# Masked attention on one core: q and k staged by token halves, the prologue by token halves, and another handling of the last two sweeps and of the fallback branch

## The reference

```python
def reference(x, adj, Wq, bq, Wk, bk, Wv, bv, Wo, bo):      # x (8, 1024, 512) f32, adj (8, 1024, 1024) int32
    h = maximum(layernorm(x), 0)
    q, k, v = heads(h @ Wq + bq), heads(h @ Wk + bk), heads(h @ Wv + bv)      # 16 heads of 32
    scores = einsum('bhqd,bhkd->bhqk', q, k) / sqrt(32)
    scores = where(adj[:, None] == 0, -inf, scores)
    out = einsum('bhqk,bhkd->bhqd', softmax(scores), v)
    return x + out.transpose(0, 2, 1, 3).reshape(b, s, 512) @ Wo + bo
```

## Time and profile before

| | |
|---|---|
| median of 3 runs | 1936.64 us (1936.35 to 1942.9) |
| the profiled execution, time | 1935.79 us |
| its span | 1933.9 us |
| PE busy | 1854.5 us, 96% |
| DVE, ACT, POOL busy | 79%, 76%, 82% |
| DMA queue of SP | 203.47 MB, 38.1% of 16 engines |

### The profile page before, as it was taken

One profiled execution on the slowest core, in us unless ns is written; L12 is line 12 of the kernel. 1 busy time (PEld: TensorE's weight loads), 2 busy tenths in 40 slices (PEclk: granted clock), 3 DMA queues, 4 the chain that ended last, 5 costly groups with the idle time before them and its releaser, 6 DMA issues.

```text
span 1933.9 us, 35135 instructions
## 1 busy us (share of the span) xinstructions
PE 1854.5 (96%) x13856; PEld 767.9 (40%) x13856; DVE 1534.0 (79%) x1585; ACT 1473.5 (76%) x1772; POOL 1588.5 (82%) x701
## 2 busy tenths in 40 slices
PE   6989999999999999999999999999999999999997
PEld 4334434444344443444433443334344344343432
DVE  6788877887778887788877887778877788777775
ACT  4878886788867988678876788768887688867763
POOL 0988888887987979878889788888889889898873
PEclk9999999999999999999999999999999999999999
DMA  7532363523615335143442335423444224443121
GB/s 236 141 79 75 97 155 88 138 69 98 167 55 142 88 107 156 50 126 93 134 123 75 101 109 133 117 86 88 113 128 131 82 77 120 137 115 97 35 55 45
DMA packets 114136, 206.09 MB, mean 107 GB/s; under 512 B 12848, under 2 KB 16048, under 8 KB 113968
## 3 DMA queue, kind: packets, MB, share of 16 engines
q1 hardware_dynamic: 113104, 203.47, 38.1%
q10 hardware_dynamic: 864, 0.34, 0.1%
HBM read 153.43 MB, written 50.33 MB: 105 GB/s over the span
## 4 chain that ended last, share of the span: by engine, by line
PE 80%; DVE 10%; DMA 4%; ACT 3%; issue 2%; POOL 0%; SPq 0%; DVEq 0%; POOLq 0%; ACTq 0%
PE ps L783 21%; PE ps L770 20%; PE ps L738 14%; PE ps L820 8%; DVE ring L1068 8%; PE ps L752 7%; PE ps L745 7%; DMA k_stack<-k_parts 2%; ACT ring L905 1%; DMA k_parts<-k_part 1%; PE ps L734 1%; PE ps L793 1%; DVE oT_lo L1125 1%; ACT mask L966 1%; DMA ring<-x 0%
## 5 line engine op out<-in xcount | busy, mean ns | idle before, releaser
L1068 DVE TENSOR_TENSOR ring<-ps,mask 128x1024 f32<-128x1024 f32 x1024 | 1217.3, 1217 | 333.2 <-PE ps L770 306.5
L905 ACT ACTIVATE ring<-ring 128x1024 f32<-128x1024 f32 x1024 | 1062.4, 1050 | 236.1 <-DVE ring L1068 225.6
L1285 POOL TENSOR_TENSOR acc<-acc,ring 128x1024 f32<-128x1024 f32 x380 | 902.8, 2403 | 0.4 <-ACT ring L905 0.4
L1285 POOL TENSOR_TENSOR acc<-ring 128x1024 f32<-128x1024 f32 x252 | 608.8, 2427 | 305.0 <-ACT ring L905 300.4
L770 PE MATMUL ps<-q_stack,k_stack 128*128 128x512 f16 x2048 | 608.0, 382 | 49.3 <-DVE ring L1068 38.9
L783 PE MATMUL ps<-ring,v_sb 128*32 128x512 f32 x4096 | 505.9, 600 | 0.0
L770 PEld LDWEIGHTS ps<-q_stack,k_stack 128*128 128x128 f16 x2048 | 157.6, 97 | 415.9 <-DVE ring L1068 232.5
L783 PEld LDWEIGHTS ps<-ring,v_sb 128*32 128x32 f32 x4096 | 107.2, 109 | 263.2 <-issue 232.9
L820 PE MATMUL ps<-acc,ones 128*32 128x512 f32 x1008 | 131.3, 593 | 0.5 <-POOL acc L1285 0.5
L933 ACT ACTIVATE rden<-ps 128x512 f32<-128x512 f32 x64 | 38.3, 598 | 114.1 <-PE ps L820 114.1
L745 PE MATMUL ps<-wv_lo,hT_hi 128*128 128x128 f16 x1024 | 100.3, 219 | 0.0
(11 more groups left out here) (88 smaller groups left out, 1565.4 us busy)
## 6 DMA issues: line engine op xcount, KB each, us to landing
x_in<-x SPq DMA_DIRECT2D x172, 256.0 KB, 2.9
edges<-adjT SPq DMA_DIRECT2D x128, 256.0 KB, 3.8
q_stack<-q_parts SPq DMA_DIRECT2D x124, 256.0 KB, 4.8
k_stack<-k_parts SPq DMA_DIRECT2D x124, 256.0 KB, 4.8
q_parts<-q_part SPq DMA_DIRECT2D x64, 256.0 KB, 2.0
k_parts<-k_part SPq DMA_DIRECT2D x64, 256.0 KB, 2.1
out<-x_in SPq DMA_DIRECT2D x60, 256.0 KB, 2.0
ring<-x SPq DMA_DIRECT2D x4, 512.0 KB, 5.4
```

What stands on the lines that cost most here:

```text
L905: nc.scalar.activation(tile, tile, ACT.Exp, scale=SCALE / UP / UP).then_inc(s["prob_ready"], 1)
L1068: nc.vector.tensor_tensor(ring[:, slot_of(kt, pair), :].rearrange("p (a n) -> p a n", n=HALF), ps_s(j), mask[:, kt:kt + 1, half * HALF:(ha ...
L1285: nc.gpsimd.tensor_tensor(acc[:, group, pair, :], first_of, ring[:, slot_of(kt, pair), :], ALU.add).then_inc(s["sum_done"], 1)
```

## The change

Four parts.

1. **Prologue by token halves.** SP asks for x tiles 0 to 3, Wq, Wk, x tiles 4 to 7, Wv, a mask tile, bo (which leaves ACT's queue), three mask tiles. Statistics, means, rstd, normalising, transposes and projections are done for tokens 0 to 511 and then for 512 to 1023. `early_pair` puts the products with w_lo of q and k behind the other eight groups.
2. **q and k by token halves in every unit.** Each half is stored when its high or low part is there and loaded back by itself: 16 loads of 128 KB and 8 stores of 128 KB in a unit where there were 8 loads and 4 stores of 256 KB. PE waits for the first halves ahead of tile 0, for the second half of k ahead of tile 8, and for the second half of q ahead of tile 16. `PRODUCTS` and the lags of `high` and `low` are as before.
3. **The last two sweeps.** Sweep 62 has POOL's groups A and B again and `BLOCKS` as any other. Sweep 63 has the terms A, 6, 7 and B, where B is kt 4 and 5. Two additions of bo move from tiles (3, 8), (3, 9) to (2, 14), (2, 15). The reduction of `limits` stays ahead of POOL's sums of tile 12.
4. **One block.** The second block is gone: each engine waits for the flag, reads it and branches behind its own work; SP waits for its last stores (`landed`) behind that.

```diff
@@ general_attention
-        block = ctx.enter_context(nc.Block())
-
         def gated(eng, program):
+
+            eng.wait_ge(verdict_taken, 4)
             wanted = eng.value_load(flag, min_val=0, max_val=1)
             with eng.If(wanted > 0):
                 program()
...
             gated(sp, program)
+            landed(sp)
@@ tables
-LAST_BIAS_AT = {(1, 24): 4, (1, 25): 5, (3, 8): 6, (3, 9): 7, (3, 14): 0, (3, 15): 1, (3, 24): 2, (3, 25): 3}
-
-LAST_TERMS = "A4567"
-UNIT_BLOCKS = {6: ("p0", "p1"), 10: ("p2", "p3"), 14: ("p4", "p5", "dA", "d4", "d5"), 18: ("p6", "d6", "p7", "d7")}
-LAST_BLOCKS = {6: ("p0", "p1"), 10: ("p2", "p3"), 14: ("p4", "p5", "dA", "d4", "d5"), 16: ("p6", "d6"), 17: ("p7", "d7")}
+LAST_BIAS_AT = {(1, 24): 4, (1, 25): 5, (2, 14): 6, (2, 15): 7, (3, 14): 0, (3, 15): 1, (3, 24): 2, (3, 25): 3}
+
+LAST_TERMS = "A67B"
+LAST_SUMS_AT = 8
+LAST_BLOCKS = {6: ("p0", "p1"), 10: ("p2", "p3"), 14: ("p4", "p5", "dA"), 16: ("p6", "d6"), 17: ("p7", "d7", "dB")}
...
 def terms_of(V):
-    return LAST_TERMS if V >= LAST_SWEEP - 1 else TERMS
+    return LAST_TERMS if V == LAST_SWEEP else TERMS
...
 def blocks_of(V):
-    return BLOCKS if V < LAST_SWEEP - 1 else UNIT_BLOCKS if V < LAST_SWEEP else LAST_BLOCKS
+    return BLOCKS if V < LAST_SWEEP else LAST_BLOCKS
@@ SP
+            def store_half(kind, hl, half):
+                tokens = slice(half * HALF, (half + 1) * HALF)
+                sp.dma_start(parts[kind][:, hl, tokens], part[kind][:, hl, tokens]).then_inc(s[f"{kind}_{('high', 'low')[hl]}_{half}_stored"], 16)
+
+            def load_half(U, kind, hl, half):
+                tokens = slice(half * HALF, (half + 1) * HALF)
+                sp.wait_ge(s[f"{kind}_{('high', 'low')[hl]}_{half}_stored"], 16 * (U + 1))
                 for quarter, which in enumerate({"q": (0, 1, 0, 1), "k": (0, 0, 1, 1)}[kind]):
                     if which == hl:
+                        sp.dma_start(stack[kind][quarter * DH:(quarter + 1) * DH, U % 2, :, tokens],
+                                     parts[kind][:, hl, tokens].rearrange("(h p) n -> p h n", h=HG))\
+                            .then_inc(s[kind + "_second_half_stacked" if half else "first_half_stacked"], 16)
...
+            load_x_first(0)
+            load_x_first(1)
             load_weights(0)
             load_weights(1)
+            load_x_first(2)
+            load_x_first(3)
+            load_weights(2)
             load_edges(0, 0)
+            sp.dma_start(bo_row[:], bo.partition_broadcast(P)).then_inc(s["const_loaded"], 16)
...
                         for g, u, kind, t in [c for c in HIGH_AT.get(G - 3, ()) if c[2] in "qk"]:
-                            if t == 1:
-                                load_stack(unit_no(g, u) + 1, (u + 1) % 2, kind, 0)
+                            load_half(unit_no(g, u) + 1, kind, 0, t)
@@ PE
+                if j == 0:
+                    pe.wait_ge(s["first_half_stacked"], 16 * 8 * (U + 1))
+                elif j == QT:
+                    pe.wait_ge(s["k_second_half_stacked"], 16 * 4 * (U + 1))
+                elif j == SWEEP:
+                    pe.wait_ge(s["q_second_half_stacked"], 16 * 4 * (U + 1))
...
+            def early_pair(t):
+                banks = {kind: early_bank(PRO_CHUNKS.index((kind, t))) for kind in "qk"}
+                for kind in "qk":
...
+                    pe.wait_ge(s["w_hi_ready"], "qk".index(kind) + 1)
                     pe.wait_ge(s["high_ready"], ...)
+                    products(kind, t, 0, 0, DC, banks[kind], None)
                     pe.wait_ge(s["low_ready"], ...)
+                    products(kind, t, 0, DC, 2 * DC, banks[kind], None)
+                for kind in "qk":
                     pe.wait_ge(s["w_lo_ready"], "qk".index(kind) + 1)
+                    products(kind, t, 0, 2 * DC, 3 * DC, banks[kind], None).then_inc(s["chunk_ready"], 1)
@@ ACT, prologue
-            rstds(0)
+            rstds(1, slice(0, QT // 2))
             weights_high(0)
             for t in range(QT // 2):
                 early_high("t", t)
             weights_high(1)
+            act.wait_ge(s["const_ready"], 5)
+            early_high("q", 0)
+            rstds(2, slice(QT // 2, QT))
+            early_high("k", 0)
+            square(PRO_CHUNKS.index(("q", 0)), "q", 0, None)
+            square(PRO_CHUNKS.index(("k", 0)), "k", 0, None)
             for t in range(QT // 2, QT):
                 early_high("t", t)
...
             weights_high(2)
...
             early_high("q", 1)
@@ DVE, prologue
-            for t in range(QT):
+            for t in range(QT // 2):
                 statistic(None, True, 0, t)
-            means(0)
-            for t in range(QT):
+            means(QT // 2, range(QT // 2))
+            for t in range(QT // 2):
                 normalise_first(t)
...
             for t in range(QT // 2):
                 early_low("t", t)
             weights_low(0)
...
+            statistic(None, True, 0, 4)
+            statistic(None, True, 0, 5)
             weights_low(1)
             dve.wait_ge(s["const_ready"], 5)
             early_low("q", 0)
+            statistic(None, True, 0, 6)
+            statistic(None, True, 0, 7)
+            means(QT, range(QT // 2, QT))
             early_low("k", 0)
+            for t in range(QT // 2, QT):
+                normalise_first(t)
             for t in range(QT // 2, QT):
                 early_low("t", t)
             weights_low(2)
@@ POOL
-                        if last and up == UNITS - 1 and j % SWEEP // PAIRS >= 4:
+                        if last and up == UNITS - 1 and j >= SWEEP + 12:
                             continue
```

More of the change, by code:

```diff
@@ L18, with general_attention @@
 AX = mybir.AxisListType
-def general_attention(nc, flag, x, adj, Wq, bq, Wk, bk, Wv, bv, Wo, bo, ident, out, scratch):
+def general_attention(nc, block, landed, verdict_taken, flag, x, adj, Wq, bq, Wk, bk, Wv, bv, Wo, bo, ident, out, scratch):
     qT_s, kT_s, v_s, o_s = scratch
@@ L437, in two_before, with fast_attention @@
     return SEQUENCE[i - 2] if i >= 2 else None
-def fast_attention(nc, x, adjT, Wq, bq, Wk, bk, Wv, bv, Wo, bo, ident, headones, out, parts, flag):
+def fast_attention(nc, outer, block, x, adjT, Wq, bq, Wk, bk, Wv, bv, Wo, bo, ident, headones, out, parts, flag):
     ctx = ExitStack()
@@ L608, in _ @@
-            load_first("k", 1)
+            for half in range(2):
+                for kind in "qk":
+                    sp.wait_ge(s["high_ready"], PRO_CHUNKS.index((kind, half)) + 1)
+                    store_half(kind, 0, half)
+                    sp.wait_ge(s["low_ready"], LOWS_BEFORE[kind, half])
+                    store_half(kind, 1, half)
+                    if half == 1:
+                        i = "qk".index(kind)
+                        sp.wait_ge(s["mask_ready"], i + 1)
+                        load_edges(0, i + EDGE_SLOTS)
+                for kind in ("qk", "kq")[half]:
+                    for hl in range(2):
+                        load_half(0, kind, hl, half)
@@ L687, in _ @@
                 sp.dma_start(out_t[B - 1, t], x_last(t)).then_inc(stored[t % X_SLOTS], 16)
-            for k in range(X_SLOTS):
-                sp.wait_ge(stored[k], 16 * B * QT // X_SLOTS)
         @block.tensor
@@ L881, in _ @@
             pe.wait_ge(s["ident_loaded"], 16)
-            for kind, t in PRO_CHUNKS[:QT + 4]:
-                early(kind, t)
+            for half in range(2):
+                for t in range(half * QT // 2, (half + 1) * QT // 2):
+                    early("t", t)
+                early_pair(half)
             pe.wait_ge(s["const_loaded"], 16 * 2)
@@ L1176, in graph @@
                             weights_low(3)
-                        if j == SCALE_O_AT and not (first and up == 0):
+                        if j == (LAST_SCALE_O_AT if last and up == UNITS - 1 else SCALE_O_AT) and not (first and up == 0):
                             scale_o(U - 1, 1)
-                        if j == SWEEP + SCALE_O_AT:
+                        if j == SWEEP + (LAST_SCALE_O_AT if last and up == UNITS - 1 else SCALE_O_AT):
                             scale_o(U, 0)
@@ L1199, in graph @@
                             if (up, j) == MEANS_AT:
-                                means(b + 1)
+                                means((b + 2) * QT, range(QT))
                             if (up, j) == SHIFT_AT:
@@ L1320, in _, with landed @@
             graph(B - 1, False, True)
+        def landed(sp):
+            for k in range(X_SLOTS):
+                sp.wait_ge(stored[k], 16 * B * QT // X_SLOTS)
+        return landed, s["verdict_step"]
 def program(nc, x, adj, adjT, Wq, bq, Wk, bk, Wv, bv, bv_cols, Wo, bo, ident, headones, out):
```

162 lines of the change are left out of this document (59 added, 103 removed).

## The result

The changed kernel takes 1940.66 us, the median of 22 runs (1939.30 to 1943.53). The kernel before, run as often on the same chips, takes 1935.49 us (1929.99 to 1945.15). The ratio is 1.0029, with a 95% interval from 1.0020 to 1.0038: 5.2 us more in the medians, inside the half per cent that the prediction called no change, though the whole interval lies above one: a small loss is measured. The profiled execution took 1940.56 us with a span of 1938.6, 4.7 us over the span before.

The account below looks back on a forecast made before the run. PE, busy 229.9 of a batch's 234.9 us, was taken to bound the kernel. The terms 1.0 - 6.4 + 10.5 - 4.6 = +0.5 us on 1935.79 gave 1936.3, or 1937.1 as median of runs; range 1932 to 1944.

Parts of the forecast that it names:

- Prologue: +1.0 forecast: Up to the first score tile: by token halves it comes 1.0 us later, with bounds of -1 and +2.7.
- The chain up to DVE's last low: Prologue, DVE's queue in the new order: the last low ends at 30.7 us where it ended at 29.0.
- the added wait on ACT: Prologue: ACT runs the second rstd ahead of k's high, which, ready since 22, runs only from 24.0 to 24.7 us.
- at full clock 35.1, at half clock 36.8: Prologue: time in us of the first score tile if PE's clock stays at 1.00, or if idle time brings half clock.
- q and k by halves: -6.4 forecast: In the batches: all six of PE's waits for k's stack go, -6.4 us, or -3 if half of it stays.
- nothing takes their place at once, since DVE and ACT stood idle there: At the batches' waits for k's stack: no other wait replaces the six removed, so all 6.4 us are gained.
- The worry that was priced, SP's queue: Rival: 12 more issues a unit take 10 us of SP's queue and make it late, costing 12 us: 1949; chance 0.06.
- The last two sweeps: +10.5 forecast: Last unit: fewer denominator terms, but PE waits for POOL's sums behind the reduction; +10.5 us, bounds +9 and +13.
- a wait of "about 13 us" for `acc`: Last unit, dB of sweep 62: PE waits about 13 us for POOL's sums of tiles 12 and 13.
- the rival that only the way to it costs: Last unit: POOL loses 5.54 + 0.44 us at the reduction, none behind it; +3.1 in place of 10.5, 1929.7; chance 0.09.
- One block: -4.6 forecast: Tail: PE reads the flag and branches behind its last product, without a second block; -4.6 us, bounds -2.6 and -5.4.
- the last landing as what sets the end in that case: Tail: if PE's queue branches ahead of its products' end, the last landing sets the end at about 1928.5, -5.4 us.

Follow-up runs that it names:

- e6: The change with its last two sweeps as before, plus 20 products that nobody reads ahead of the prologue's second four transposes: 1927.05 us, ratio 0.9953 to the kernel before.
- e10: The change with POOL's reduction last, term B's denominators behind tile 7's, and the 20 unread products in the prologue: 1918.61 us, ratio 0.9912 to the kernel before.
- e11: The same three edits as e10, on the change with its last two sweeps as before: 1922.34 us, ratio 0.9933 to the kernel before.
- e2: The change with its last two sweeps and its prologue as before, leaving q and k by halves and one block: 1926.96 us, ratio 0.9958 to the kernel before.
- e5: e2 with term B's denominators placed behind those of tile 7 in each sweep: 1924.82 us, ratio 0.9936 to the kernel before.
- e7: The change with POOL's reduction of the limits left out, a subtraction in its place: 1925.47 us, ratio 0.9945 to the kernel before.
- e3: The kernel before with only q and k by token halves in every unit: 1929.78 us, ratio 0.9981 to the kernel before.
- e12: The kernel before with only POOL's reduction and the steps behind it moved to the end: 1934.57 us, ratio 0.9977 to the kernel before.
- e1: The change with only its last two sweeps as before: 1932.01 us, ratio 0.9980 to the kernel before.

## Why the prediction was right, and which of its terms were not

The forecast was 1937.1 us with no change that can be told as the likeliest. The kernel takes 1940.7: inside the range and inside 0.5%, but 3.6 us above the forecast. Most mechanisms that were named are in the trace, and two that were not named are there too: a wait for POOL at the batches' ends, and a late landing at the end. The terms were these.

**Prologue: +1.0 forecast, +2.55 in the trace, bounds -1 to +2.7.** The chain up to DVE's last low was right to 0.2 us: forecast 30.7, found 30.87, with the added wait on ACT at its place. So was what stands behind it: at full clock 35.1, at half clock 36.8. I took a value between the two; it was the half clock, and 0.7 us more (37.51), since the half clock began ahead of the transposes and the group of products before the low parts was slow as well. The edit of e6 shows that it is the clock: every new prologue without the added products has its first score tile at 36.7 to 38.0, and with them it stands at 34.0 to 34.1 in e6, e10 and e11. The idle time of 4.24 us ahead of the transposes was in the working; it should have decided the choice. The old prologue had its half clock in three of six traces (before, e2, e5), so +2.55 is the price against one execution that had some of it.

**q and k by halves: -6.4 forecast, -3.1 in the batches, bounds -6.4 to -3.** The number is inside its bounds, but not for the reason that they were given: no wait for the stack stayed. The six waits went as forecast. The step that failed is "nothing takes their place at once, since DVE and ACT stood idle there": true of DVE and ACT, but POOL was not asked about. It is busy for 200 of a batch's 235 us, and its last sum comes 0.44 us after PE now wants it. e5 shows it: with that term asked for later, the batch shrinks from 234.44 to 233.8 us. POOL's six waits are 2.6 of the 3.3 us that are missing; the other 0.7 are not placed. The worry that was priced, SP's queue, did not come: its waits for ACT's masks fell from 198.2 us to 131.5 and stayed far from nothing, and its waits for the landing of a store of k rose from 27.4 to 89.4 us, with nobody waiting for SP. Whether the longer waits of SP cost anything in the prologue was not tried.

**The last two sweeps: +10.5 forecast, +8.5 in the trace, bounds +9 to +13.** A wait of "about 13 us" for `acc` was forecast and 12.69 was found; POOL's gaps of 5.5 and 7.1 us stood where they were expected, as 5.57 and 7.09. e7 shows that both belong to the reduction, and the rival that only the way to it costs (the Trainium skill, GPSIMD Engine Reference, Instruction dispatch, names about 6 us, for a first call) falls on the second gap. The 5.57 us ahead of the reduction agree with that page; the 7.09 behind it are not in it. Against the execution from which the forecast was made the term is 2 us too large, and just outside its bounds: behind that place PE had waits of its own before, of 2.25 and 2.13 us for DVE, which shrank to 0.24 and 1.67, and 3.4 us of half clock (granted clock 0.76 and 0.90 in 1890 to 1895 and 1895 to 1900), which are gone. The delay took these in; the forecast added it to a path that had slack of its own. That slack is not the kernel's in every execution, as the last unit's 58.8 us in e2 and e3 show, and the medians give 8.6 and 12.6 us, one on each side of the forecast. The size was right as far as it can be told.

**One block: -4.6 forecast, -3.3 in the trace, bounds -2.6 to -5.4.** PE's branch was hidden better than the forecast had it: PE's queue ran ahead of its products by 3 us. The forecast had the last landing as what sets the end in that case, but at its old 2.2 us; it took 4.5, and that is the step that was mis-sized.

Together 2.55 - 3.1 + 8.5 - 3.3 = 4.65 us, against 4.7 in the spans. Two terms were too favourable by 1.5 and 3.3, one too unfavourable by 2.0, and the tail by 1.3 too favourable: 4.1 us above the sum of +0.5. Being within 0.5% is not owed to the one error that went the other way: with 10.5 us for the last sweeps the sum would be 6.7, still under the 9.7 us of that limit. That the miss is 4.1 us and not 6 is owed to it.

The gain of the change went into a wait of its own making, the 12.7 us at dB and the half clock behind it, and none of that is needed. With the reduction last the same change is 9 us faster than before.

## What to carry to other kernels

When a wait is removed, ask of every engine, not only of those next to the wait, when it is due next: the one that is 85% busy is the one that takes the gain back. A reduction over partitions on POOL should stand behind the last sum that anybody waits for, and not two tiles later in the same queue. When two changes meet, take the price of each with and without the other: here one pair of runs gave 8.6 us and another 12.6 for the same edit. Where PE must stand for some microseconds ahead of critical products, either give it products without a reader or count those products at half clock.

## What the hardware showed that I had not expected

- The reduction over partitions has a record of 0.44 us and takes POOL for 13.1: 5.4 to 6.2 us ahead of it and 6.7 to 7.6 behind it, in every kernel where something stands behind it. A simple subtraction at its place costs 0.22 and no gap.
- At half clock PE's 16 transposes of f32 in the prologue take 3.67 us, and with the clock at 1.00 they take 2.09 (e6).
- The branch on the flag costs PE's queue 3.5 to 5.2 us and the other queues 0.05 to 0.07. PE's queue takes it up to 3 us ahead of the end of its running products.
- With the branches behind the last work the slowest store of the tail lands after 3.7 to 4.7 us; with them in a block of their own after 2.2.
- Strays: in three of the twelve profiled executions a DVE instruction (two in e12), each time the low part of the outputs, took 8.6 to 8.7 us where the others of that line take 1.5:

```profile
1349.34 8.63 DVE L1128 SCALAR_TENSOR_TENSOR oT_lo<-o_raw,b_up,oT_hi 128x1024 f16<-128x1024 f32 x1
```

It cost PE a wait of 6.3 us. This one is e1's; the others are in e6 and e12, at other times of the run. What causes it is not known. Whether it also explains the runs without a profile that lie some 7 to 10 us above the rest is not shown. A trace that holds one should not be used for a difference of a few microseconds across it.
